# Moving the values product of a cross-attention kernel behind the squares product, into another PSUM bank

## The reference

```
x = x + xattn(layernorm(x), ctx_1024)
x = x + ffn(layernorm(x))

xattn(h, c):
    q = rmsnorm(h @ Wq) * gq     # per head, (B, 100, 16, 128)
    k = rmsnorm(c @ Wk) * gk     # per head, (B, 361, 16, 128)
    v = c @ Wv
    attn = softmax(q k^T / sqrt(128))
    return (attn v) @ Wo

ffn(h):
    gate, up = hbitlinear(h, w_gate), hbitlinear(h, w_up)
    return hbitlinear(silu(gate) * up, w_down)
    # hbitlinear: Hadamard rotation, 8-bit rows, ternary weights
```

## Time and profile before

| | us |
|---|---|
| median of 3 runs | 1381.54 (1379.87 to 1381.78) |
| the profiled execution, its own time | 1381.65 |
| its span, first to last instruction | 1379.8 |
| TensorE matmul busy | 1359.2 (99%) |
| VectorE busy | 917.1 (66%) |
| ScalarE busy | 918.1 (67%) |
| GpSimd busy | 540.6 (39%) |
| granted TensorE clock | 1.00 of full speed (2.4 GHz) |

### The profile page before, as it was taken

How to read it: one execution, slowest core, us unless ns; L and a number is a source line. 1 busy time by engine, 2 the same in 40 slices (tenths; PEclk the granted TensorE clock), 3 DMA queues, 4 the chain that set the end, 5 groups by cost and what they waited for, 6 DMA issues and landing times. The chain is left out here.

```text
span 1379.8 us, 28300 instructions
## 1 busy us (share of the span) xinstructions
PE 1359.2 (99%) x9496; PEld 1212.2 (88%) x9496; DVE 917.1 (66%) x2414; ACT 918.1 (67%) x2019; POOL 540.6 (39%) x477
## 2 busy tenths in 40 slices
PE   9999989999999999999999999999999999999997
PEld 9899867999999999999999999998978887888885
DVE  6312046667777777777777777766558778887886
ACT  5556568878888888888888888787734433444342
POOL 1034326433233323323332423324735555555551
PEclk9999999999999999999999999999999999999999
DMA  8867813333444444444434443434462342334212
GB/s 250 234 186 202 231 55 111 110 105 110 135 114 129 120 120 120 140 114 117 138 113 122 129 120 118 121 102 137 153 189 55 90 88 62 70 76 102 62 32 43
DMA packets 186403, 166.36 MB, mean 121 GB/s; under 512 B 87938, under 2 KB 155540, under 8 KB 184468
## 3 DMA queue, kind: packets, MB, share of 16 engines
q1 hardware_dynamic: 178980, 151.50, 39.9%
q10 hardware_dynamic: 7280, 13.06, 3.6%
HBM read 124.57 MB, written 33.02 MB: 114 GB/s over the span
## 5 line engine op out<-in xcount | busy, mean ns | idle before, releaser
L804 POOL TENSOR_TENSOR rk_sp<-ms_sp,neg_half 124x6 f32<-124x6 f32 x128 | 169.8, 1354 | 465.9 <-DMA ms_sp<-ms 465.9
L1237 DVE CUSTOM_DVE_ANT_0 sc<-psS,rk 100x361 f32<-100x361 f32 x256 | 136.6, 533 | 131.4 <-PE psS L889 92.8
L1032 ACT ACTIVATE pr<-ex,ri 100x361 f32<-100x361 f32 x256 | 152.5, 596 | 42.8 <-DVE ri L1225 42.8
L1025 ACT ACTIVATE ex<-sc,nb,rq_all 100x361 f32<-100x361 f32 x256 | 174.8, 683 | 2.9 <-DVE nb L1246 2.9
L917 PE MATMUL psZ<-pT_hi,cK_hi 120*128 120x400 f32 (+1 forms) x384 | 132.7, 346 | 0.0
L917 PE MATMUL psZ<-pT_hi,cK_lo 120*128 120x400 f32 (+1 forms) x384 | 132.1, 344 | 0.0
L917 PE MATMUL psZ<-pT_lo,cK_hi 120*128 120x400 f32 (+1 forms) x384 | 131.9, 344 | 0.0
L1007 ACT ACTIVATE ring_hi<-bank 128x362 fp32r<-128x362 f32 x128 | 60.5, 473 | 77.8 <-PE bank L865 77.0
L902 PEld LDWEIGHTS psP<-ident,pr 100*120 100x120 f32 (+1 forms) x768 | 73.5, 138 | 43.5 <-issue 35.3
L1217 DVE TENSOR_TENSOR pT_lo<-psP,pT_hi 122x600 fp32r<-122x600 f32 x128 | 98.9, 773 | 1.2 <-ACT pT_hi L1056 1.1
L932 PE MATMUL psNV<-z,wv_sb 128*128 128x200 f32 x504 | 97.2, 336 | 0.8 <-issue 0.8
(11 more groups left out here) (315 smaller groups left out, 3895.9 us busy)
## 6 DMA issues: line engine op xcount, KB each, us to landing
rk<-rk_dram SPq DMA_DIRECT2D x128, 290.6 KB
q_dram<-q_out SPq DMA_DIRECT2D x64, 200.0 KB, 4.4
q_in<-q_dram SPq DMA_DIRECT2D x64, 200.0 KB, 3.9
o_dram<-o SPq DMA_DIRECT2D x64, 200.0 KB, 4.3
stage<-in_w_ff SPq DMA_DIRECT2D x12, 1024.0 KB, 6.4
w_in<-in_w_ff ACTq DMA_DIRECT2D x48, 256.0 KB, 3.9
o_in<-o_dram SPq DMA_DIRECT2D x12, 1024.0 KB, 5.9
cT_in<-in_ctxT SPq DMA_DIRECT2D x15, 361.0 KB, 4.0
```

Of the source, the lines that this page charges most:

```text
L804: nc.gpsimd.tensor_tensor(rk_sp[:, cols], ms_sp[:, cols], neg_half[0:HG * SKR, :].to_broadcast([HG * SKR, n]), op=ALU.pow).then_inc(g_rk, 1)
L1025: nc.scalar.activation(ex[:, h % 2, :], sc[:, h % 2, :], ACT.Exp, bias=nb[:, h % 2:h % 2 + 1], scale=factor(n), accum_out=rs[:, h % 2:h % ...
L1032: nc.scalar.activation(pr[:, h, SKP - SK:SKP], ex[:, h % 2, :], ACT.Copy, scale=ri[:, h % 2:h % 2 + 1]).then_inc(a_pr, 1)
L1237: nc.vector.tensor_tensor_reduce(out=sc[:, h % 2, :], in0=psS[0:SQ, 0:SK], in1=rk[:, u % 2, h, 0:SK], scale=1.0, scalar=-3.0e38, op0=ALU.m ...
```

## The change

- `values` runs one unit later, `values(u-4)`, in slot 0 directly behind `squares(u+2)` and ahead of the transposes, and writes `psZ[1]`, the bank of the second gather half. `psNV` is left to the squares, whose only wait on that bank is now for `mean_squares` (`v_ms`).
- `gather(u-2, 1)`, whose bank is `psZ[1]`, is issued in two parts: six matmuls in slot 1 and three in slot 2. The first part now also waits for `copy_o` of the values before it (`a_o`).
- ScalarE's `copy_o` moves from slot 3 to the head of slot 1, VectorE's `copy_z` from slot 2 to slot 3, and SyncE stores `o` one unit later.
- `values` waits for the `copy_z` of the gather half that had its bank; no longer for `v_ms`, but at the end.
- At the end the last two values products are issued together in slot 3 of unit 65, the first of them into `psNV`.

```diff
@@ SyncE
-                if real(u - 3, UNITS):
-                    store_o(u - 3)
+                if real(u - 4, UNITS):
+                    store_o(u - 4)
                 if u == UNITS + 1:
+                    store_o(UNITS - 2)
                     store_o(UNITS - 1)
@@ TensorE, squares
                 pe.wait_ge(a_k, u * HG + HG)
-                if due(u - 5):
-                    pe.wait_ge(a_o, u - 5)
+                if due(u):
+                    pe.wait_ge(v_ms, u)
@@ TensorE, gather and values
-            def gather(u, c):
+            def gather(u, c, chunks=range(3)):
...
-                if due(u):
+                if due(u) and chunks[0] == 0:
                     pe.wait_ge(v_z if c else a_z, u)
-                n = 0
-                for i in range(3):
+                if c == 1 and due(u - 1) and chunks[0] == 0:
+                    pe.wait_ge(a_o, u - 1)
+                n = chunks[0] * 3
+                for i in chunks:
...
-                last.then_inc(p_z, 1)
+                if n == 9:
+                    last.then_inc(p_z, 1)
...
             def values(v, bank):
                 first = v // 2 * 2
                 pe.wait_ge(a_z, first + 2)
-                pe.wait_ge(v_z, first + 2)
-                pe.wait_ge(v_ms, min(v + 6, UNITS))
+                pe.wait_ge(v_z, min(v + 2, UNITS))
+                if v >= UNITS - 2:
+                    pe.wait_ge(v_ms, UNITS)
@@ TensorE, unit
                     if h == 0 and real(u + 2, UNITS):
                         squares(u + 2)
+                    if h == 0 and real(u - 4, UNITS):
+                        values(u - 4, psZ[1])
                     if h == 0 and real(u - 1, UNITS):
                         transposes(u * 2 - 1, 1)
+                    if h == 1 and real(u - 2, UNITS):
+                        gather(u - 2, 1, range(0, 2))
+                    if h == 2 and real(u - 2, UNITS):
+                        gather(u - 2, 1, range(2, 3))
                     if h == 2 and real(u, UNITS):
                         transposes(u * 2, 0)
-                    if h == 2 and real(u - 3, UNITS):
-                        values(u - 3, psNV)
-                    if h == 2 and u == UNITS + 1:
+                    if h == 3 and u == UNITS + 1:
+                        values(UNITS - 2, psNV)
                         values(UNITS - 1, psK[1])
                     if h == 3 and real(u - 1, UNITS):
                         gather(u - 1, 0)
-                    if h == 1 and real(u - 2, UNITS):
-                        gather(u - 2, 1)
@@ ScalarE, unit
+                    if h == 1 and real(u - 4, UNITS):
+                        copy_o(u - 4, psZ[1])
...
-                    if h == 3 and real(u - 3, UNITS):
-                        copy_o(u - 3, psNV)
                     if h == 3 and u == UNITS + 1:
+                        copy_o(UNITS - 2, psNV)
                         copy_o(UNITS - 1, psK[1])
@@ VectorE, unit
-                    if h == 2 and real(u - 2, UNITS):
+                    if h == 3 and real(u - 2, UNITS):
                         copy_z(u - 2)
-                    if h == 2 and u == UNITS + 1:
+                    if h == 3 and u == UNITS + 1:
                         first_norm()
```

## The result

| | before | after |
|---|---|---|
| median, us | 1381.78 (21 runs) | 1384.57 (21 runs) |
| ratio, 95% interval | | 1.0020 (1.0014 to 1.0026) |
| profiled execution, its own time | 1381.65 | 1383.68 |
| span | 1379.8 | 1381.9 |

The changed kernel is 2.8 us slower, 0.20%. One of its 21 runs took 2149.62 us, at a mean granted clock of 0.578, and is left out of the ratio.

A forecast was written before the change was run, and what follows sets the result against it. TensorE's steps were taken to bound attention. Seams of -0.3 us plus 0 for moved steps, on the profiled 1381.65 us, gave 1381.3 us; own range 1378.8 to 1384.3, widened to 1378.4 to 1385.0.

The forecast's parts named there:

- What bounds the kernel: In attention TensorE never waits, so the time is the sum of its steps, 12.4 us a unit on average.
- the signs of being wrong: Steady matmuls released by `pr`, `o` or `ring_lo`; first-to-last scores moving over 3 us; another cost for the seam behind squares.
- the short units: Units 61 to 65, without keys: the gather may wait for `copy_o`; taken as 0, ends -0.2 and +1.5 us.
- Squares to values: New seam in slot 0, 58 times: 0.075 us in place of 0.055, +1.2 us; ends -3.2 and +2.6.
- The yardstick: First value after a wait, its load uncovered: 0.41 us against 0.333, taken as the price of squares to values.
- Squares to transposes: Existing seam once a unit, first transpose 304 ns against a median of 249: 0.055 us, removed by the change.
- Transposes to values: Existing seam in slot 2, first value 358 ns against 333: 0.025 us, removed 61 times, -1.5 us.
- The sum of seams: All seams between kinds of matmul on TensorE together: 1.2 - 1.5 = -0.3 us.
- The rule on loads by columns: Skill's rule that load time goes by columns: a value's open load about equals a transpose's, seams then -1.5 us.
- The moved steps: Values, `copy_o`, gather parts, slot 2 transposes, `copy_z`, `store_o`: each hidden or on time in steady units, cost 0.
- The rival on the other side: ScalarE waiting before `copy_o` makes `pr` late for slot 2 transposes: +4.0 us (1385.3) or +6 (1387), chance 0.13.
- the upper end of a cost that I had named: Squares to values at 0.10 us, +2.6 us, with a wait in the short units: adds 0.02 to slower's chance.

The follow-up runs named there:

- e5: Kernel before with one swap in slot 2, values ahead of transposes: ratio 0.9991 to the kernel before, period 12.532 us.
- e3: Changed kernel with the second gather half whole again in slot 1 and `copy_z` back in slot 2: ratio 1.0014 to the kernel before, period 12.592 us.
- e7: Changed kernel with values ahead of squares in slot 0 (values, squares, transposes), gather still cut: ratio 0.9996 to the kernel before, period 12.542 us.
- e11: Changed kernel with values ahead of squares in slot 0 and the gather whole in slot 1: ratio 1.0003 to the kernel before, period 12.548 us.
- e12: Kernel before with values ahead of transposes in slot 2, the same arrangement as e5 measured again: ratio 0.9988 to the kernel before, period 12.532 us.
- e4: Kernel before with one swap in slot 0, transposes ahead of squares: ratio 1.0016 to the kernel before, period 12.590 us.

## Why the prediction was wrong

- **What bounds the kernel**: right. TensorE's steps in another order, 100.00 busy before and after. But of the signs of being wrong that I had named, only one caught the loss. No matmul of the steady stretch is recorded as waiting. The distance from first to last scores moved by 1.3 us (790.6 to 792.0), under my 3 us, since it holds the head start of 1.7 us as well as the steady 2.5 and the 0.5 of the short units. The seam behind the squares did cost something else.
- **Squares to values, "I take 0.075"**: the step that failed. It measured 0.104 us, at my upper bound: 58 x (0.104 - 0.052) = +3.0 us in place of +1.2. The yardstick was right, its reading was not: I took the excess of the matmul's duration, and its load had begun 0.03 us before it. The first key of the earlier trace rows, a load of the same 128 columns with load and matmul recorded together, had the right size, 0.10, and I kept it for the bound. The loads of the earlier trace rows gave it too: a value's is recorded 0.052 us longer than a transpose's (190 against 138 ns), and 0.055 + 0.052 = 0.107.
- **Squares to transposes, 0.055**: 0.052.
- **Transposes to values, 0.025**: mis-sized a little the other way. e5 takes this seam out alone, gains 0.0275 a unit and shortens the first value's step by 0.027; -1.7 us in place of -1.5.
- **The sum of seams, "-0.3 us"**: with the measured sizes it is +1.3 us. The measured steady loss is 2.5. So the mis-sized seam is 1.8 us of the error and not all of it. The other 1.2 us of the steady loss is in steps that I put at nothing: by the starts of all matmuls in the 57 units, those of the scores are longer by 0.013 us a unit and those of the gather by 0.007. About 0.7 us comes and goes with the cut between the change and e3, but e7 against e11 does not confirm it. It is not chance of one execution, since e5 and e12 agree; its cause stays open.
- **The rule on loads by columns, weighed and found not to agree**: it was right that the trace disagreed, since a transpose's load is the odd one out, but I drew the wrong thing from it. The open loads measured are 0.104 us for a value (128 columns) and 0.08 for a score (100 columns). The Trainium skill ("TensorE: Matmul & The Clock Gate", LDWEIGHTS) gives a load as its columns over 1.2, in ns: 107 and 83, an estimate that agrees with both; for a transpose's 122 columns it would be 102, and the runs show 52. With its 107 the seams would have come to +1.5 us or so beforehand.
- **The moved steps**: right in the steady units. `copy_o` waits 0.63 us, and no matmul of TensorE is recorded as idle for it, for `pr` or for the scaling of the scores; the step ahead of the transposes of slot 2 is 0.182 us, as between two gather matmuls. The short units had a wait on `copy_o`, 0.5 us, and took 0.5 us longer in all, within the 0 to 1.5 that I allowed.
- **The rival on the other side** (probabilities late through `copy_o`) did not occur. The loss came from the upper end of a cost that I had named, to which I had given 0.02. Forecasting "same" with a term known only to 0.1 us and multiplied by 58 was too sure: 2.6 us above was in my own bounds. That the stage came out at just +2.6 is partly luck, since part of it is the shifts that I had not priced.

## What to carry to other kernels

On an engine that is never idle, an order of work is priced by its seams: find, for each kind of matmul, what its weights cost to load when nothing covers them, and let the kind with the cheapest open load follow whatever leaves it uncovered, as the squares do here. Values of 0.169 us a step belonged ahead of transposes of 0.086, not behind them (e5). And read an uncovered load from the start of the load to the second matmul, less a usual step, not from the first matmul's duration.

## What was unexpected about the hardware

- Behind the squares, four products side by side on column strips, the next load is not hidden, whichever of three kinds it was: 0.052 us for a transpose, 0.08 for a score, 0.104 for a value, at the full clock. Each is some 0.085 us less than the recorded duration of that load (138, 164 and 190 ns), so the profile's duration of a load is not its price, but the difference of two is the difference in price. Ahead of them another 0.09 us goes (keys to squares: the step is 0.255 instead of 0.165), behind keys, transposes (e4) and values (e7) alike.
- The load of a 100 x 122 transpose costs half of what its columns would make it by the two others.
- The steps of unchanged matmuls (keys, gather, scores) shift by up to 0.015 us a unit with the arrangement around them, the same in two executions of one arrangement. What causes it stays open.
